# Third attention of a four-block image kernel: 32-pixel cells packed into groups of the array, and the norm's sums from products

## The reference

```python
q, k, v = conv3x3(x, Wq), conv3x3(x, Wk), conv3x3(x, Wv)
att = einsum('nchw,mchw->nmhw', q, k) / sqrt(128)   # 16 x 16 images, at each pixel
att = softmax(att, axis=1)
virt = einsum('nmhw,mchw->nchw', att, v)
mu, var = mean(virt, (1, 2, 3)), var(virt, (1, 2, 3))   # one pair per image
virt = relu((virt - mu) * rsqrt(var + 1e-5) * gamma + beta)
return x + conv3x3(virt, Wc)
```

## Time and profile before

| | |
|---|---|
| Median of three runs | 554.14 us |
| The profiled execution, its time and its span | 552.4 us, 550.6 us |
| PE, busy share | 85% |
| VectorE (DVE), busy share | 63% |
| ScalarE (ACT), busy share | 48% |
| GpSimd (POOL), busy share | 24% |

### The profile page before, as it was taken

The page is one execution under the profiler, slowest core; times in us unless marked ns, Lnnn a source line. Parts: engine busy times, 40 slices in busy tenths (PEclk is TensorE's granted clock), DMA queues, the critical chain, the costliest instruction groups (busy, mean ns, idle before and its releaser), DMA issues.

```text
span 550.6 us, 10106 instructions
## 1 busy us (share of the span) xinstructions
PE 470.5 (85%) x3522; PEld 363.9 (66%) x3522; DVE 348.1 (63%) x895; ACT 262.7 (48%) x654; POOL 134.0 (24%) x161
## 2 busy tenths in 40 slices
PE   4286797879998999899889989999998999884995
PEld 3163564556776768676767766676766788784885
DVE  1418844872868577556867775776538343666896
ACT  3332665743554464435454635533444431994541
POOL 5210563242103102110220022111101111512672
PEclk9997786967999999699999989996998899996999
DMA  6000111000000000000000000000000000004112
GB/s 208 19 19 2 43 44 63 0 21 19 2 1 21 20 1 19 19 0 0 19 19 0 0 19 0 0 20 2 1 1 19 2 20 1 2 1 152 40 38 76
DMA packets 9486, 13.15 MB, mean 24 GB/s; under 512 B 496, under 2 KB 8816, under 8 KB 9328
## 3 DMA queue, kind: packets, MB, share of 16 engines
q1 hardware_dynamic: 9456, 12.76, 7.0%
HBM read 8.56 MB, written 4.19 MB: 23 GB/s over the span
## 4 chain that ended last, share of the span: by engine, by line
PE 57%; DVE 17%; ACT 10%; issue 8%; POOL 4%; DMA 4%; DVEq 0%; SPq 0%; ACTq 0%; POOLq 0%
PE bank L1199 7%; PE bank L1201 5%; PE bank L1200 5%; PE bank L1312 5%; PE bank L1394 5%; PE bank L1368 4%; DMA w_stage<-convs 4%; PE bank L1366 2%; PE bank L1344 2%; PE bank L1422 2%; PE bank L1228 2%; ACT x L798 2%; PE bank L1381 2%; ACT prob L740 1%; DVE even L892 1%
## 5 line engine op out<-in xcount | busy, mean ns | idle before, releaser
L1199 PE MATMUL bank<-win,w_hi 128*128 128x256 f32 x384 | 122.3, 318 | 12.3 <-DVE win L1145 5.9
L740 ACT ACTIVATE prob<-bank 128x512 f32<-128x512 f32 x128 | 69.5, 596 | 95.4 <-PE bank L1366 94.7
L1200 PE MATMUL bank<-win,w_hi 128*128 128x256 f32 x384 | 109.4, 285 | 0.0
L1201 PE MATMUL bank<-win,w_lo 128*128 128x256 f32 x384 | 109.3, 285 | 0.0
L992 DVE TENSOR_REDUCE nmax<-bank 128x2 f32<-128x512 f32 x128 | 85.3, 685 | 34.3 <-PE bank L1344 33.9
L1199 PEld LDWEIGHTS bank<-win,w_hi 128*128 128x128 f32 x384 | 74.0, 193 | 23.7 <-issue 10.8
L1200 PEld LDWEIGHTS bank<-win,w_hi 128*128 128x128 f32 x384 | 74.1, 193 | 0.7
L1201 PEld LDWEIGHTS bank<-win,w_lo 128*128 128x128 f32 x384 | 73.7, 192 | 0.0
L517 POOL TENSOR_TENSOR first<-first 128x256 f32<-128x256 f32 x24 | 17.7, 737 | 174.6 <-ACT first L629 174.6
L1368 PE MATMUL bank<-qk 32*128 32x256 f32 x256 | 43.9, 357 | 4.3 <-ACT prob L740 3.8
L1368 PEld LDWEIGHTS bank<-qk 32*128 32x128 f32 x256 | 26.4, 204 | 19.6 <-issue 6.9
(11 more groups left out here) (235 smaller groups left out, 930.4 us busy)
## 6 DMA issues: line engine op xcount, KB each, us to landing
w_stage<-convs SPq DMA_DIRECT2D x4, 576.0 KB, 4.8
x_in<-x SPq DMA_DIRECT2D x8, 256.0 KB, 2.6
out<-x_pair SPq DMA_DIRECT2D x8, 256.0 KB, 2.2
q<-out SPq DMA_DIRECT2D x1, 2048.0 KB, 8.3
out<-v SPq DMA_DIRECT2D x8, 256.0 KB, 2.1
cst<-small SPq DMA_DIRECT2D x1, 1708.0 KB, 9.7
cst<-small SPq DMA_DIRECT2D x1, 253.5 KB, 2.9
```

The source lines that it names most:

```text
L740: act.activation(prob[:, x // 4 % 2, x % 4, :, :], bank[ST_BANK[x % 2]][:, :], ACT.Exp, scale=L2_SCALE).then_inc(st_exp, 1)
L1199: mm(dst, hi, x_hi, start=(row == 0), stop=False)
L1200: mm(dst, hi, x_lo, start=False, stop=False)
L1201: return mm(dst, lo, x_hi, start=False, stop=(row == KH - 1))
```

## The change

The pixels are cut into cells of two pixels by 16 images, 32 columns. For a cell the product is 32 by 32. Four cells are put side by side in the array: the products of q and k go to four groups of 32 columns (all 128 channels on the rows), the products with v to four groups of 32 rows, each into a bank of its own. All logits fit in two banks; the softmax runs in two halves of 512 columns, and all its steps but the exponential are VectorE's. The cells pick every fourth column of `q3` and `k3`, and the products with v write every fourth column of their bank. The convolutions of the last pair run in the order v, q, k, all before the attention; v is transposed between them. The norm's sums come from PE: the sum over all tiles of `virt` transposed by itself (its diagonal, the squares) and of `virt` times a column of ones. The reload of `x3_back` waits for the products of q and k instead of the last total.

```diff
+TILES = HW // GPX
+BANDS = 4
+ROWS = TILES // BANDS
+HALF = ROWS // 2
+GROUPS3 = GPX // 2
+CELL = 2 * N
+LAST_ORDER = (2, 0, 1)
+        def cells(t):
+            return t[:, :].rearrange("p (b T i g) -> p b T g i", b=ROWS, T=BANDS, i=CELL, g=GROUPS3)
+        def pv3_bank(h, T):
+            return ((2, 3, 4, 5), (0, 1, 6, 7))[h][T]
@@ SP
-            sp.wait_ge(tot3_done, BATCHES)
+            sp.wait_ge(dot3_done, 2)
@@ GpSimd: the multiplication by the inverse sums is gone
-            for b in range(BATCHES):
-                pool.wait_ge(att3_inv_done, b + 1)
...
@@ ScalarE
+            for b in range(ROWS):
+                if b == ROWS // 2:
                     first_copy(PAIRS - 1, 2)
+                v3t_copy(b)
+            for h in range(2):
+                act.wait_ge(att3_sub, h + 1)
+                act.activation(att3[h], logit3[h], ACT.Exp).then_inc(att3_exp, 1)
+            for h in range(2):
+                act.wait_ge(att3t_done, h + 1)
+                act.activation(att3_t[:, h, :], bank[6 + h][:, :], ACT.Copy).then_inc(att3t_copied, 1)
+            for h in range(2):
+                act.wait_ge(virt_done, h + 1)
+                for T in range(BANDS):
+                    act.activation(virt...[:, T, h * HALF:(h + 1) * HALF, :],
+                                   bank[pv3_bank(h, T)]..., ACT.Copy).then_inc(virt_copied, 1)
@@ VectorE
+            for h in range(2):
+                dve.wait_ge(dot3_done, h + 1)
+                dve.scalar_tensor_tensor(cell(logit3[h]), cell(bank[h][:, :]), L3_SCALE, mask, ...)
+                dve.tensor_reduce(nmax3[:, h, :], cell(logit3[h]), X, ALU.max, negate=True)
+                dve.tensor_tensor(cell(logit3[h]), cell(logit3[h]), spread(nmax3, h), ALU.add)
+            for h in range(2):
+                dve.wait_ge(att3_exp, h + 1)
+                dve.tensor_reduce(att3_sum[:, h, :], cell(att3[h]), X, ALU.add)
+                dve.reciprocal(att3_inv[:, h, :], att3_sum[:, h, :])
+                dve.tensor_tensor(cell(att3_n[h]), cell(att3[h]), spread(att3_inv, h), ALU.mult)
+            dve.wait_ge(gram_done, 1)
+            dve.tensor_tensor(gram, bank[2][:, 0:P], c("ident"), ALU.mult)
+            dve.tensor_copy(sum3[:, 0:1], bank[3][:, 0:1])
+            dve.tensor_reduce(sum3[:, 1:2], gram, X, ALU.add)
+            for k in range(2):
+                dve.tensor_scalar(spread3[:, k, :], c("same_n"), sum3[:, k:k + 1], None, ALU.mult)
+            dve.wait_ge(tot3_done, 1)
@@ TensorE
+            def dots(h):
+                for b in range(HALF):
+                    for T in range(BANDS):
+                        o = (b * BANDS + T) * CELL
+                        for g in range(GROUPS3):
+                            ins = mm(bank[h][g * CELL:(g + 1) * CELL, o:o + CELL], cells(q3)[:, h * HALF + b, T, g, :],
+                                     cells(k3)[:, h * HALF + b, T, g, :], start=True, stop=True)
+                ins.then_inc(dot3_done, 1)
+            def attended(h):
+                pe.wait_ge(att3_scaled, h + 1)
+                for b in range(HALF):
+                    ins = tr(bank[6 + h][:, b * P:(b + 1) * P], att3_n[h][:, b * P:(b + 1) * P], ident)
+                ins.then_inc(att3t_done, 1)
+                pe.wait_ge(att3t_copied, h + 1)
+                for b in range(HALF):
+                    for g in range(GROUPS3):
+                        for T in range(BANDS):
+                            r = slice(T * CELL, (T + 1) * CELL)
+                            dst = bank[pv3_bank(h, T)][:, :].rearrange("p (b i g) -> p b g i", b=HALF, g=GROUPS3)
+                            ins = mm(dst[:, b, g, :], v3_t[r, h * HALF + b, g, :],
+                                     att3_t[r, h, b * P + g * CELL:b * P + (g + 1) * CELL], start=True, stop=True)
+                ins.then_inc(virt_done, 1)
+            convolve(PAIRS - 1, 0, 3 * UNITS)
+            units = 3 * UNITS
+            for b in range(ROWS):
+                convolve(PAIRS - 1, units, units + 2)
+                units += 2
+                v3_transposed(b)
+            convolve(PAIRS - 1, units, GROUPS * UNITS)
+            pe.wait_ge(joined, 3 * PAIRS)
+            pe.wait_ge(v3t_copied, ROWS)
+            for h in range(2):
+                dots(h)
+            for h in range(2):
+                attended(h)
+            for b in range(BANDS * 2):
+                h, T = divmod(b, BANDS)
+                pe.wait_ge(virt_copied, b + 1)
+                for t in range(HALF):
+                    o = ((h * HALF + t) * BANDS + T) * P
...
+                    mm(bank[2][:, 0:P], virt[:, o:o + P], virt[:, o:o + P], start=first, stop=last)
+                    ins = mm(bank[3][:, 0:1], virt[:, o:o + P], ones_r[:, 0:1].bitcast(F32), start=first, stop=last)
+            ins.then_inc(gram_done, 1)
+            pe.wait_ge(spread3_done, 2)
+            mm(bank[4][:, 0:2 * N], c("mean_all"), spread3[:, :, :], start=True, stop=True).then_inc(tot3_done, 1)
```

More of the change, by code:

```diff
@@ L556, in _ @@
             first_sum(PAIRS - 2, 2)
[L557 removed]
+            for w in range(3):
                 first_sum(PAIRS - 1, w)
[L560 to L569 removed]
             for g, cols in enumerate(LN_GROUPS):
@@ L782, in _ @@
             window_high(PAIRS - 1, 1)
-            first_copy(PAIRS - 1, 0)
-            first_copy(PAIRS - 1, 1)
+            for w in range(2):
+                first_copy(PAIRS - 1, w)
             def v3t_copy(b):
                 act.wait_ge(v3t_done, b + 1)
[L787 to L803, removed]
-                    first_copy(PAIRS - 1, 2)
[L805 to L817, removed]
+                act.activation(v3_t[:, b, :, :].rearrange("p g c -> p (g c)"), bank[4 + b % 2][:, :],
+                               ACT.Copy).then_inc(v3t_copied, 1)
@@ L1087, in _ @@
             join(PAIRS - 2, 2)
[L1088 to L1118, removed]
-            dve.wait_ge(tot3_done, BATCHES)
@@ L1120, in _ @@
-            dve.tensor_copy(tmv3[:, :, :].rearrange("p k n -> p (k n)"), bank[0][:, 0:2 * N]).then_inc(ln_chain, 1)
+            for w in range(3):
+                join(PAIRS - 1, w)
+            mask = c("mask3").unsqueeze(1).to_broadcast([P, HALF * BANDS, CELL])
+            cell = lambda t: t.rearrange("p (t x) -> p t x", x=CELL)
+            spread = lambda t, h: t[:, h, :].unsqueeze(2).to_broadcast([P, HALF * BANDS, CELL])
+            for h in range(2):
+                dve.wait_ge(dot3_done, h + 1)
+                dve.scalar_tensor_tensor(cell(logit3[h]), cell(bank[h][:, :]), L3_SCALE, mask, ALU.mult,
+                                         ALU.add).then_inc(logit3_done, 1)
+                dve.wait_ge(logit3_done, h + 1)
+                dve.tensor_reduce(nmax3[:, h, :], cell(logit3[h]), X, ALU.max, negate=True).then_inc(nmax3_done, 1)
+                dve.wait_ge(nmax3_done, h + 1)
+                dve.tensor_tensor(cell(logit3[h]), cell(logit3[h]), spread(nmax3, h), ALU.add).then_inc(att3_sub, 1)
```

110 lines of the change are left out of this document (41 added, 69 removed).

## The result

The changed kernel takes 584.57 us (median of four runs, 579.65 to 586.06); the kernel before took 555.03 us on the same chip. The ratio is 1.057 [1.051, 1.063]: 29.5 us slower. The forecast was 565, and the range ended at 582. The profiled execution took 586.06 us with a span of 584.0; before it was 552.4 and 550.6. Every ratio here leaves out slow runs, those more than 1.5% above the fastest of the same kernel (one of e11 took 2224.91 us).

A forecast was written before the change was run, and what follows sets the result against it. PE, 85% busy, was taken to bound the kernel. Convolutions, transposes, products, pause, sums and clock put the norm's totals at 511.0 against 499.35, +11.6 us: 564.0 from the profiled run, 565.7 by the median, given as 565; range 555 to 582.

The forecast's parts named there:

- the clock: After the softmax pause: PE's clock falls to half for one 4 us stretch in the products with v, 2.0 us lost.
- the products with v: Attention's second products: 256 instructions, four row groups running together, 7.0 us in all, 3.5 us a half.
- the pause: Softmax between the two sets of products: PE stands still 3.9 us with nothing covering it.
- the sums: Norm's sums on PE: 128 instructions at 0.11 us, a single column costing as much as 128; 14.1 us.
- The third rival: Short products keep the clock at 1.2 GHz from the products of q and k on; 585 us, chance 0.10.
- bound of 22 us: Upper bound on the clock's loss, if it stays low from the first product to the last sum.
- 547: Time in us of the rival with short products nearly free and no clock lost; chance 0.12.
- 572: Time in us if groups run two at a time in the products with v, 14.8 instead of 7.0; rival's chance 0.18.
- Products of q and k: Attention's first products: 256 instructions in four column groups, 64 rounds each waiting a load; 7.0 us, bounds 3.2 to 11.8.
- The first rival: Attention and sums: short products nearly free, loads hidden, single columns vanish; 5.1 us faster than before, chance 0.12.
- Stride: Transposes of v reading every fourth column: bound 0 to 3.5 us more, taken at 0.
- The reload: Reload of 2 MB, 8.3 us, moved up under the attention; costed at nothing, earlier landing gives nothing.

The follow-up runs named there:

- e11: e7 with v's last four transposes between blocks of the first half's products with v, the second half's attention transposed after that half; ratio to before 1.011.
- e1: Changed kernel plus 27 unused convolution matmuls in PE's softmax pause and 9 while ScalarE copies the transposes; ratio to before 1.057.
- e9: Changed kernel plus 36 unused convolution matmuls ahead of the norm's sums; 573.59 us, one run.
- e2: Changed kernel without the first 31 single-column products of the sums (mean then wrong); ratio to before 1.027.
- e3: Changed kernel with the sums in two passes, all single-column products first, then all squares; 576.63 and 585.57 us.
- e4: Changed kernel's attention with the norm of before (squares on ScalarE, sums on VectorE); ratio to before 1.018.
- e6: Changed kernel with cells, transposes and results in unbroken runs instead of every fourth column (result permuted); 586.31 us, one run.
- e7: Changed attention with the old norm, reordered: all convolutions, products of q and k, v's transposes in the pause, products with v unbroken; ratio to before 0.995.
- e8: e7 plus two extra 128 by 128 products (results overwritten) before each of eight blocks of products with v; ratio to before 1.000.

## Why the prediction was wrong

**The step that failed** is the clock: "I take one such low stretch of 4 us in the products with v, 2.0 us lost." The fall in the pause came as said. What was wrong is the return: the one I had seen came after 4.0 us of dense convolutions, and I took it for what any continuous work of PE does. e1 shows that under 32-column products even a full clock falls, e9 beside the changed kernel that the mix of full and single columns keeps the clock it finds, e2 and e3 that 128-column products by themselves raise it. What about the products or the sums makes the difference these runs don't separate further. The low stretch was 58 us, 484.5 to 542. Against the forecast it cost 13.3 us in the sums and, beyond the 2.0 counted, 5.2 in the products with v; together that is a little more than the whole error of 17.9 us (29.5 measured, 11.65 forecast), the products of q and k having come out 1.4 lower. The third rival had the mechanism, with the price of 585 us and a chance of 0.10; its bound of 22 us stood in my own text, against 2.0 in the sum. It had the start too early by one stage: the products of q and k ran at full clock. So its price was too high for the stretch, 32.1 us more than before against 29.5, and that its 585 meets the measured 584.57 is in part luck. (This price, like 547, 572 and the 558 to 572 of the forecast's own range, starts from 564.0, the forecast 565 from 565.7; the 1.7 us change nothing here.)

**The prices were right** at the clock they were made for: 3.70 us for a half of the products with v (e1) where I had 3.5, 0.109 us per instruction of the sums (e9) where I had 0.11, a pause of 3.8 for 3.9. With both at full clock the stretch would be 29.5 - 13.4 - 2 x 3.35 = 9.4 us longer than before (an estimate), near the 9.65 that I had without the clock.

**Products of q and k**: 5.6 for 7.0. Their pace, 4.34 us for 253 instructions, 0.017 each, lies under the 0.0275 that I took from loads; 0.94 us of "issue" gave part of it back. In the five other profiles of the same products (e1, e2, e3, e4, e9) they took 6.2 to 6.5 us, with 1.2 to 1.6 us of "issue".

**The first rival** (short products nearly free) was out in its largest term: single columns cost as much as full ones (e2, e3), and PE was on the path with every one of them. In the products of q and k it was half right, 4.7 us of PE between its 3.2 and my 7.0. **Stride** cost 0.4 us instead of a bound of 3.5 (e6). **The reload** landed 9.1 us after its issue, well under the attention, and gained nothing: 51.34 us after the mark against 51.25.

**What the change could give**, then. In the attention of the form before PE was busy for 8.6 us with the products of q and k, 8.7 with those with v and 5.0 with the attention's transposes. In cells these are 4.7, 2 x 3.70 (e1) and 2 x 0.66 us at full clock, 9 us less. The sums take that back and more, 14.0 us where adding the totals had been 2.7, and PE's new pause of 3.8 us comes on top. ScalarE's busy time fell from 262.7 to 245.4 us and VectorE's from 348.1 to 336.2, but their work had run beside PE's; on this path it bought little. e7, with the old norm and the pause mostly filled, is what is left: 3.5 us in the stretch.

## What to carry to other kernels

Before pricing a stage of small or single-column products, ask for both clocks: which one it will find, and whether its own work raises, keeps or drops it; a busy share doesn't answer that. In these traces the low stretch ended under full products (convolutions, or 128 by 128 by themselves), so price the low clock up to there. And where other engines' work that ran mostly under cover is moved to the engine on the path, its full price counts, here 128 x 0.11 us for the sums.

## What I had not expected of the hardware

- The same 128 instructions of the sums took 27.4 us or 14.0 us by the clock found at their start (after, e9), in both cases with PE busy throughout.
- 32-column products in four groups let a full clock fall with PE at 100%: after 3.7 us in e1, after 4.6 us in e7. With two 128 by 128 products per block the clock stayed full for 13.4 us (e8).
- Turning two loops made the products with v 3.6 times as slow (25.03 against 7.05 us).
- At 0.015 to 0.017 us an instruction PE stood still for no reason that the profile shows: 1.23 and 1.80 us of "issue" in e6, 0.94 in the changed kernel.
